# A mixture-of-experts layer on one core: picks ordered by expert number, expert rows reloaded in two halves, and two tiles' rows added by TensorE

## What is computed

```
x'     = x @ W.T + b + 2 * (x @ A[slot]) @ B[slot]            # per sequence of 32 tokens
scores = softmax(x' @ router_w + router_b) + router_bias      # 16 experts, 4 groups of 4
idx    = the 2 best experts of a token, from the 2 best groups
y      = sum over the 2 picks of score * ((silu(x' @ w1 + b1) * (x' @ w2 + b2)) @ w3 + b3)
z      = (silu(x' @ sw1 + sb1) * (x' @ sw2 + sb2)) @ sw3 + sb3   # shared expert
out    = x + y + z
```

## Time and profile before

| | |
|---|---|
| median of 3 runs | 169.54 us (169.12 to 170.14) |
| profiled execution, its own time | 169.93 us |
| its span, first to last instruction | 168.2 us |
| mean granted TensorE clock | 0.973 |
| busy, PE / DVE / ACT / POOL | 147.6 / 97.6 / 58.7 / 57.6 us |
| all blocks scattered, reload begins | 146.6 us into the span |

### The profile page before, as it was taken

The page is one execution under the profiler, slowest core; times in us unless marked ns, Lnnn a source line. Parts: engine busy times, 40 slices in busy tenths (PEclk is TensorE's granted clock), DMA queues, the critical chain, the costliest instruction groups (busy, mean ns, idle before and its releaser), DMA issues.

```text
span 168.2 us, 2537 instructions
## 1 busy us (share of the span) xinstructions
PE 147.6 (88%) x742; PEld 114.9 (68%) x743; DVE 97.6 (58%) x231; ACT 58.7 (35%) x117; POOL 57.6 (34%) x71
## 2 busy tenths in 40 slices
PE   3899899999979999999989999999999977999100
PEld 3678688888767778887867857866777753888000
DVE  2663675558957578978128854334534533436994
ACT  4532422714622151154543423433343321026600
POOL 6810140000000020435205765665476572209700
PEclk9999999999999999999999999999999999999955
DMA  4999938999863599998301557877674452389964
GB/s 173 302 370 380 394 76 321 394 420 414 314 230 146 146 389 365 406 432 276 111 5 66 184 191 248 212 267 250 217 242 169 149 169 81 125 305 392 363 257 179
DMA packets 16507, 42.59 MB, mean 253 GB/s; under 512 B 2192, under 2 KB 2192, under 8 KB 16240
## 3 DMA queue, kind: packets, MB, share of 16 engines
q1 hardware_dynamic: 11392, 25.41, 41.5%
q0 software_dynamic: 3616, 12.06, 22.0%
q10 hardware_dynamic: 1488, 4.98, 7.5%
HBM read 33.53 MB, written 8.91 MB: 252 GB/s over the span
## 4 chain that ended last, share of the span: by engine, by line
PE 62%; DMA 13%; DVE 8%; issue 8%; POOL 4%; ACT 2%; SPq 0%; POOLq 0%; DVEq 0%
PE bank L909 29%; PE bank L1076 14%; DMA xg_sb<-xt_rows,slot_tok 6%; PE bank L1091 6%; PE bank L1066 4%; DMA condW_raw<-in_condWT 3%; PE bank L965 2%; DVE x_sb L882 2%; DMA yg_sb<-y_rows 2%; POOL yg_sb L449 2%; POOL y_rows L421 2%; PE bank L955 2%; DMA y_rows<-y_sb,slot_row 2%; PE bank L976 1%; DVE x_sb L876 1%
## 5 line engine op out<-in xcount | busy, mean ns | idle before, releaser
L1076 PE MATMUL bank<-w_sb,xgT_sb 128*128 x144 | 37.4, 383 | 1.8 <-issue 1.8
L1076 PEld LDWEIGHTS bank<-w_sb,xgT_sb 128*128 128x128 f32 x144 | 25.4, 190 | 13.2 <-issue 10.6
L421 POOL DMA_INDIRECT y_rows<-y_sb,slot_row x18 | 18.6, 1031 | 24.9 <-DVE y_sb L828 24.9
L415 POOL DMA_INDIRECT xg_sb<-xt_rows,slot_tok x20 | 19.4, 968 | 11.9 <-issue 8.0
L816 DVE TENSOR_TENSOR pre_sb<-bank,b_sb 128x256 f32<-128x256 f32 x18 | 7.6, 425 | 25.4 <-PE bank L1076 25.2
L1091 PE MATMUL bank<-w_sb,hT_sb 128*128 x36 | 18.5, 596 | 0.5 <-ACT hT_sb L567 0.5
L909 PE MATMUL bank<-condW_h,xT_h 128*128 128x512 f32 x32 | 13.4, 418 | 1.1 <-DVE condW_l L638 0.9
L828 DVE COPY y_sb<-bank 128x512 f32<-128x512 f32 x18 | 12.3, 684 | 1.5 <-PE bank L1091 1.5
L398 POOL MEMSET gate<- 128x768 f32 x1 | 0.7, 741 | 36.2 <-PE bank L976 36.2
L909 PE MATMUL bank<-xtT_h,sw_h 128*128 128x512 f32 x32 | 13.0, 407 | 0.0
L559 ACT COPY xgT_sb<-bank 128x512 f32<-128x512 f32 x18 | 10.5, 586 | 6.8 <-PE bank L1066 3.9
(11 more groups left out here) (164 smaller groups left out, 285.9 us busy)
## 6 DMA issues: line engine op xcount, KB each, us to landing
w_sb<-in_w SPq DMA_DIRECT2D x8, 1024.0 KB, 9.1
w_sb<-in_w ACTq DMA_DIRECT2D x2, 2048.0 KB, 14.5
yg_sb<-y_rows SPq DMA_DIRECT2D x8, 512.0 KB, 6.5
xt_rows<-xt_ring SPq DMA_DIRECT2D x8, 256.0 KB, 4.3
b_sb<-in_b SPq DMA_DIRECT2D x1, 2048.0 KB, 10.8
x_sb<-in_x SPq DMA_DIRECT2D x8, 256.0 KB, 2.9
out<-x_sb SPq DMA_DIRECT2D x8, 256.0 KB, 2.1
xT_raw<-in_xT SPq DMA_DIRECT2D x3, 512.0 KB, 5.0
```

Source lines behind the costliest of these rows:

```text
L415: pool.indirect_dma_start(xg_sb[:, b % 4, :], None, xt_rows, bass.IndirectOffsetOnAxis(ap=slot_tok[:, b:b + 1], axis=0)).then_inc(gathered ...
L421: pool.indirect_dma_start(y_rows, bass.IndirectOffsetOnAxis(ap=slot_row[:, b:b + 1], axis=0), y_sb[:, b % 2, :], None).then_inc(y_scattere ...
L1076: mm = pe.matmul(bank[2 + s % 2][:, 0:2 * INTER], xgT_sb[:, s % 2, k, :], w12_sb[:, bass.ds(e * W12 + k * 2 * INTER, 2 * INTER)], start=(k ...
```

## The change

Four things are changed. (1) `choose` orders a token's two picks by expert number (`pick`: minimum, maximum), so that pick 0 is the lower expert; the gates are then taken out of the scores through `sel` into `val`. (2) SP first waits for the blocks below `base[E - 1]`, the first row of expert 15, and loads pick 0 of all tiles in four DMAs of two tiles (`low_in`). It then reads the two full counts, waits for all blocks, and loads pick 1 tile by tile (`high_in`). DVE computes the new counts in six small instructions after block 3. (3) For tiles 5 and 7 PE multiplies the rows by identities scaled with the gates (`diag`, made by ACT) and accumulates into the shared product's bank. (4) ACT's scaling and POOL's adding are gone, and DVE handles the other six tiles, pick by pick, in a new order; each tile has a PSUM bank to itself.

```diff
-POOLED = (0, 1, 2, 4, 5)
-FINISHED = (0, 1, 3, 2, 4, 5, 6, 7)
+ON_PE = (5, 7)
+ON_DVE = (0, 1, 2, 3, 4, 6)
...
@@ SP
+            sp.wait_ge(low_known, 1)
+            low_e = sp.value_load(eid[0:1, LOW_EVEN_AT:LOW_EVEN_AT + 1], min_val=16 * LOW_BLOCKS // 2, max_val=16 * (BLOCKS + 1) // 2)
+            low_o = sp.value_load(eid[0:1, LOW_ODD_AT:LOW_ODD_AT + 1], min_val=16 * LOW_BLOCKS // 2, max_val=16 * BLOCKS // 2)
+            sp.wait_ge(y_scattered[0], low_e)
+            sp.sem_inc(low_stored, 1)
+            sp.wait_ge(y_scattered[1], low_o)
+            sp.sem_inc(low_stored, 1)
+            sp.wait_ge(low_stored, 2)
+            for n in range(TILES // 2):
+                sp.dma_start(yg_sb[:, 2 * n:2 * n + 2, 0, :], by_tile[0][:, 2 * n:2 * n + 2]).then_inc(low_in[n], 16)
             even = sp.value_load(eid[0:1, EVEN_AT:EVEN_AT + 1], min_val=16 * FULL // 2, max_val=16 * (BLOCKS + 1) // 2)
...
             for i in range(TILES):
-                sp.dma_start(yg_sb[:, i], y_rows[0:K * T, :].rearrange("(k i p) d -> i p k d", k=K, p=P)[i]
-                             ).then_inc(y_in[i], 16)
+                sp.dma_start(yg_sb[:, i, 1, :], by_tile[1][:, i]).then_inc(high_in[i], 16)
@@ POOL
-            for n, i in enumerate(POOLED):
-                pool.wait_ge(scaled, K * (n + 1))
-                pool.tensor_tensor(yg_sb[:, i, 0, :], yg_sb[:, i, 0, :], yg_sb[:, i, 1, :], ALU.add).then_inc(pair_added, 1)
@@ ACT
+            act.wait_ge(low_stored, 2)
+            for n, i in enumerate(ON_PE):
                 for k in range(K):
-                    act.activation(yg_sb[:, i, k, :], yg_sb[:, i, k, :], ACT.Copy, scale=best[:, i, k:k + 1]
-                                   ).then_inc(scaled, 1)
+                    act.activation(diag[:, n, k, :], ident[:], ACT.Copy, scale=val[:, k, i:i + 1]).then_inc(diag_ready, 1)
@@ DVE, choose
+                for k, order in enumerate((ALU.min, ALU.max)):
+                    then(dve.tensor_tensor(pick[:, tiles, k], best_at[:, tiles, 0], best_at[:, tiles, 1], order))
@@ DVE, behind the ranks
-            then(dve.tensor_tensor(tmp[:], sel[:, 0], over_experts(best[:, :, 0]), ALU.mult))
-            then(dve.tensor_tensor(sc1[:], sel[:, 1], over_experts(best[:, :, 1]), ALU.mult))
-            then(dve.tensor_tensor(sc[:], tmp[:], sc1[:], ALU.add))
+            then(dve.tensor_tensor(sel_sc, sel[:], sc[:].unsqueeze(1).to_broadcast([P, K, TILES, E]), ALU.mult))
+            then(dve.tensor_reduce(val[:], sel_sc, AX.X, ALU.add))
+            then(dve.tensor_tensor(sc[:], sel_sc[:, 0], sel_sc[:, 1], ALU.add))
@@ DVE, after block 3
+                if b == UNROLL - 1:
+                    then(dve.tensor_scalar(low_blocks[:], base[0:1, E - 1:E], 1.0 / P, None, ALU.mult))
...
@@ DVE, last stage
+            def add_mixed(i):
+                dve.wait_ge(mixed, ON_PE.index(i) + 1)
+                dve.tensor_tensor(x_sb[:, i, :], x_sb[:, i, :], shared_bank(i)[:], ALU.add).then_inc(acc_done, 1)
+            def add_low(i):
+                dve.wait_ge(low_in[i // 2], 16)
+                then(dve.scalar_tensor_tensor(out=x_sb[:, i, :], in0=yg_sb[:, i, 0, :], scalar=val[:, 0, i:i + 1],
+                                              in1=x_sb[:, i, :], op0=ALU.mult, op1=ALU.add))
+            def add_high(i):
+                dve.wait_ge(high_in[i], 16)
...
@@ PE, last stage
+            for i in ON_DVE:
+                shared_down(i).then_inc(shared_done, 1)
+            for n, i in enumerate(ON_PE):
+                shared_down(i)
+                pe.wait_ge(diag_ready, K * (n + 1))
+                pe.wait_ge(low_in[i // 2], 16)
+                pe.matmul(shared_bank(i)[:], diag[:, n, 0, :], yg_sb[:, i, 0, :], start=False, stop=False)
+                pe.wait_ge(high_in[i], 16)
+                pe.matmul(shared_bank(i)[:], diag[:, n, 1, :], yg_sb[:, i, 1, :], start=False, stop=True).then_inc(mixed, 1)
```

More of the change, by code:

```diff
@@ L232, in program @@
         y_scattered = [sem(f"y_scattered{s}") for s in range(2)]
-        shared_done, acc_shared, y_in = sem("shared_done"), sem("acc_shared"), [sem(f"y_in{i}") for i in range(TILES)]
+        shared_done, acc_shared = sem("shared_done"), sem("acc_shared")
+        diag_ready, mixed = sem("diag_ready"), sem("mixed")
+        low_in = [sem(f"low_in{i}") for i in range(TILES // 2)]
+        high_in = [sem(f"high_in{i}") for i in range(TILES)]
         acc_done, out_stored = sem("acc_done"), sem("out_stored")
@@ L878, in add_experts @@
-            def add_experts(i):
-                dve.wait_ge(y_in[i], 16)
-                dve.wait_ge(acc_shared, i + 1)
-                for k in range(K):
-                    ins = dve.scalar_tensor_tensor(out=x_sb[:, i, :], in0=yg_sb[:, i, k, :],
-                                                   scalar=best[:, i, k:k + 1], in1=x_sb[:, i, :],
-                                                   op0=ALU.mult, op1=ALU.add)
-                    if k < K - 1:
-                        then(ins)
-                ins.then_inc(acc_done, 1)
@@ new lines, in _ @@
+            add_shared(0)
+            add_shared(1)
+            add_low(0)
+            add_low(1)
+            add_shared(2)
+            add_low(2)
+            add_shared(3)
+            add_low(3)
+            add_shared(4)
+            add_low(4)
+            add_high(0)
+            add_high(1)
+            add_shared(6)
+            add_high(2)
+            add_low(6)
+            add_high(3)
+            add_high(4)
+            add_mixed(5)
+            add_high(6)
+            add_mixed(7)
@@ L1152, in _, with shared_down @@
             pe.wait_ge(b3s_done, 1)
-            for i in range(TILES):
-                if i >= 4:
-                    pe.wait_ge(acc_shared, i - 3)
+            def shared_down(i):
+                if shared_bank(i) in (bank[5], bank[6]):
+                    pe.wait_ge(acc_shared, 1)
                 for c in range(IC):
```

57 lines of the change are left out of this document (28 added, 29 removed).

## The result

The changed kernel took 172.75 us (median of 4 runs, 172.12 to 173.98) beside 169.57 us for the kernel before (169.12 to 170.14, 4 runs): a ratio of 1.0191 [1.0151, 1.0231]. The forecast of 167.6 us and the top of its range, 170.0, are both missed. The rival in which PE's clock falls, which the prediction put on the other side, came true. The profiled execution is the one of 173.01 us.

The account below looks back on a forecast made before the run. The end was taken to be bound by DVE, without gaps from 155.69, and its waits. Last stage -2.35 us plus +0.4 ahead gave -1.95: 167.6 us against the median, own range 166.9 to 168.3, final range 166.6 to 170.0.

Parts of the forecast that it names:

- The rival in which PE's clock falls: Last stage: PE's 3.1 us pause halves its clock; 169.3 us (chance 0.30) or 171.8 us (0.11).
- ahead of the last stage: Choose, gates and the six instructions after block 3 together cost +0.4 us, bounds 0 to 1.0.
- last stage: pick 1 of tile 5 lands: Last stage: tile 5's pick 1 rows land at 158.3, which PE's second product waits for.
- from there until PE's last product: Last stage: after 158.3 PE has 4.2 us to do and about 0.2 until the last lands, at 162.7.
- No early reload: Reload: expert 15 is empty, so pick 0 starts at 146.6, split, not advanced; rival of early reload 164.5 us, chance 0.05.
- DVE's last stage: Last stage: 12 instructions and 6 adds without POOL take 13.1 us from 150.13; this path gives back 2.5 us.
- When the rows are there: Reload: rate stays 1.355 us per load; pick 0 lands 150.13 to 154.2, pick 1 every 0.68 us; reads and issues hidden.
- PE's last stage: Last stage: PE idles 155.2 to 158.3, then works 4.2 us; PE and DVE end together, 163.4 instead of 165.75.
- both forms: Clock rival: short fall, 3 to 4 us at half rate, 169.3 us (0.30); long fall, all at half, 171.8 us (0.11).
- as long to rise as to fall: Clock rival, short form: 3 to 4 us of PE's work at half clock, costing 1.5 to 2 us; 169.3 us, chance 0.30.
- The six instructions: After block 3: bias add starts at 101.0 instead of 100.42; cost 0 to 0.6 us, taken as 0.3 us.
- `choose` and the gates: Ahead of the blocks: two more small instructions per choose, gates in three; mostly covered by idle, 0.1 us, between 0 and 0.4.

Follow-up runs that it names:

- e3: Changed kernel with both low counts taken from base[14], so pick 0 is loaded once the first 10 blocks are stored: 169.63 us, 0.9960 of the kernel before.
- e7: e6 with pick 0 loaded when the first 10 blocks are stored, as in e3: 170.62 us, 1.0049 of the kernel before.
- e6: e5 with DVE's shared adds of tiles 2 and 3 put ahead of pick 0: 169.08 us, 0.9939 of the kernel before.
- e1: Changed kernel with PE doing pick-0 products and tile 7's shared product before waiting for tile 5's pick 1: 170.22 us, 1.0008 of the kernel before.
- e11: Kernel before without POOL's and ACT's help, DVE adding all 16 rows, nothing on PE: 169.64 us, 0.9988 of the kernel before.
- e8: Kernel before with only the six small instructions added after block 3, their results unread: 171.07 us, measured once.
- e4: Changed kernel with the six small instructions moved from behind block 3 to ahead of the blocks: 171.74 us, 1.0086 of the kernel before.
- e2: Changed kernel, same order, with 16 more matmuls of unread result in PE's pause: 171.29 us, 1.0108 of the kernel before.
- e5: Changed kernel with the edits of e1 and e4 together: 168.99 us, 0.9955 of the kernel before.
- e9: Kernel before with PE adding whole rows of tiles 5 and 7, DVE the other six, loads reordered, no sorted picks or split: 168.80 us, 0.9958.

## Why the prediction was wrong

In the form of the prediction's sum, behind the first reload's issue and with that issue's own delay (us):

| term | predicted | measured |
|---|---|---|
| ahead of the last stage | +0.4 | +1.2 |
| last stage: pick 1 of tile 5 lands | 11.7 | 12.6 |
| from there until PE's last product | 4.4 | 7.4 |
| last add | 0.7 | 0.7 |
| last stage | 16.8 (-2.35) | 20.7 (+1.6) |

(Predicted 158.3, 162.7 and 163.4, less 146.63.) The miss is 0.8 + 4.0 = 4.8 us: -1.95 became +2.8. The median missed by 5.2 us; the other 0.3 to 0.4 us lie outside the span. Of the 4.0 us, 1.0 is the later landing and 3.0 the work behind it. (The prediction's own range about 167.6 was added up wrongly: its bounds give 168.5 at the top, not 168.3. That decides nothing.)

**No early reload: right.** Pick 0 was issued at 147.84, with all blocks stored. e3 and e7 show what it would have been worth. I gave it 3 us beside the forecast (164.5 against 167.6); between e6 and e7 it costs 1.1%.

**DVE's last stage: right.** 13.1 us from the first landing were forecast. In e1, where nothing of PE's disturbs it, they are 16.66 - 3.7 = 13.0 us. The whole forecast for the last stage, 16.8 us, is what e1 measures. That POOL's silence gives DVE its rates back is shown by e11 too. The Trainium skill (SBUF — State Buffer, section Who interferes with whom) says that DVE and GpSimd share a pair of ports, and that a DVE instruction with two SBUF inputs can be locked out by a GpSimd one that reads SBUF; the trace agrees: an add of two SBUF inputs took 1.76 us beside POOL and 0.63 us each without. (POOL's adds start from 151.6 to 158.3, and the last ends at 159.9: the prediction read the last start as the end. No reading hangs on it.)

**When the rows are there: off by 1 us.** Pick 1's eight loads did land 0.68 us apart, and SP's two reads and the issues were hidden. But the rate of 1.355 us a load isn't kept throughout: there are 2.3 us between the second and the third landing. This gap made tile 5's pick 1 late (12.6 instead of 11.7 us). It isn't the change's own: e8 and e11, which load as the kernel before does, have it as well. It stretched PE's pause from my 3.1 us to 4.0.

**PE's last stage: this step failed.** The forecast took PE's queued work behind tile 5's pick 1 at full clock. The 4.2 us of it took 7.4 us, since all but its last 1.3 us ran at 1.2 GHz. I had this as a rival, with the right place and the right price for it (8.4 us if all is slow), and gave both forms together 0.41. The failure is in how I weighed it. I set a pause of 3.1 us beside a fall seen after 2.9, and took that one fall for an edge. It is none: in the other traces the fall came 2.2 to 5.3 us after PE's last matmul, and in e6 within 3.2 us of a pause's start, with work in between. So a pause of 3.1 us may or may not have kept the clock; whether the late landing decided is not shown. I also took "as long to rise as to fall" for the likelier form without a row for it. Both forms exist: of the 7.4 us here 6.1 ran at half clock, in e4 3.4, and by the mean clocks one run in four of the changed kernel was of the short form. Even that run took 172.12 us, above the 169.3 I had priced, as the later landing and the cost ahead of the last stage come on top. e2 shows that the clock costs 2.7 us, and e1 that the wait need not stand ahead of that work at all: the order of PE's queue makes the long pause, and in that pause the clock falls. The Trainium skill (TensorE: Matmul & The Clock Gate, section Why this matters for your kernels) says that a pause of PE between bursts drops its clock mid-kernel; by this the trace agrees, and the page weighed against the forecast rightly.

**The six instructions: the term that was mis-sized.** 0.3 us, with a bound of 0.6, became 1.1 us at PE's turn (102.94 against 101.83), and 1.2 to 1.4 us over the two steps (e8: 1.4). The working was of the right kind (six waits, then two register reads, then the bias add), but it ended at 101.0, and it is 101.80. Of the two register reads one took 0.56 us, not 0.3. And the slack, of which I said that no row gives it, is only 0.3 us: before, `h_sb` was there 0.3 us ahead of the turn on PE, as this timeline of DVE in e5 has it again (101.68 + 0.29, PE's turn at 102.3):

```profile
100.88 0.42 DVE L841 TENSOR_TENSOR pre_sb<-bank,b_sb 128x256 f32<-128x256 f32 x1 [1.33 <-PE bank L1107]
101.68 0.29 DVE L846 TENSOR_TENSOR h_sb<-gl_sb,pre_sb 128x128 f32<-128x128 f32 x1 [0.38 <-ACT gl_sb L578]
```

So the other 1.1 us of the bias add's 1.38 came through. In the changed kernel's own trace a part of this hides in the pause of PE that e4 speaks of. e8 (added alone) and e5 (moved away) settle the size from both sides: 1.2 to 1.4 us.

**`choose` and the gates: right, as far as one trace can say.** The timeline of DVE in the third and fourth call:

```profile
60.05 0.19 DVE L690 TENSOR_REDUCE red<-bank 128x2 f32<-128x32 f32 x1
...
63.00 0.19 DVE L713 TENSOR_TENSOR chosen<-sel 128x32 bf16<-128x32 f32 x1
...
72.82 0.19 DVE L793 CAST slot_pair<-bank 128x32 int32<-128x32 f32 x1 [0.22 <-PE bank L1088]
```

DVE's 0.51 us of waiting ahead of L690 took up the third call's, and `slot_pair` starts at 72.82, 0.48 us earlier than before. No cost is to be seen. But block 2's down product starts anywhere from 93.2 to 94.4 us in the traces, whatever the kernel, so a term of 0.1 us can't be told from nothing.

What remains of the change when both faults are mended (e5, e6) is 0.4 to 0.6%, and e9 has as much without sorted picks. That is at the edge of what counts as a change. The part that gains is PE's sharing of the additions with POOL silent (POOL's silence alone, e11, gains nothing); the sorted picks and the split reload gain nothing here. Of the 2.35 us that the last stage should give, its length shows 1.9 in e5 and the median 0.8; the late reload and the crowded stores, told there, are the rest in the one trace, and how much of each is in every run isn't settled.

## What to carry to other kernels

Where an engine's queue holds a wait for a late load, put in front of it all work that doesn't need that load: it shortens the pause, mostly keeps the clock, and takes the work off the end (here 4.1 us off the last stage and 3.1 off the time, for one added line). One fall of the clock in one profile gives no safe length for a pause: here it came anywhere from 2.2 to 5.3 us after PE's last matmul. When a forecast has a pause of PE of that order with work behind it that the end waits for, and loads decide how long it is, treat the fall as the likelier case, and price it by the longer of the two stretches seen here, 6.1 us at half rate. Small instructions ahead of a register read on a chain that an engine waits for can cost more than they take: six in a row, 1.0 us from the first start to the last end, came to 1.2 to 1.4 us, and to nothing ahead of the loop.
